# First-layer products of the coupling net: from f32 to three f16 passes, with the low part made on VectorE

## The reference

```python
def _coupling_net(h, w1, b1, w2, b2, w3, b3, w4, b4):
    h = _gelu(h @ w1 + b1)           # 128 -> 128
    h = _gelu(h @ w2 + b2)           # 128 -> 64
    h = _gelu(h @ w3 + b3)           # 64 -> 32
    return jax.nn.sigmoid(h @ w4 + b4)   # 32 -> 1
...
gf = _global_net(x.mean(axis=1, keepdims=True), ...)
out = x
for _ in range(3):
    tf = _coupling_net(out, ...)
    combined = 0.7 * gf + 0.3 * tf
    coupling = 0.1 + adaptive_range * (combined - 0.5) * 2.0
    out = out + coupling * _twist(out)   # [p_r, -p_i, -o_r, o_i]
```

## Time and profile before

| | us |
|---|---|
| median of 3 runs | 1114.27 |
| the profiled execution | 1111.88 |
| its span, first to last instruction | 1110.2 |
| TensorE busy (matmuls) | 987.5 (89%) |
| VectorE busy | 778.4 (70%) |
| ScalarE busy | 643.7 (58%) |
| GpSimd busy | 397.7 (36%) |

### The profile page before, as it was taken

The page is one execution under the profiler, slowest core; times in us unless marked ns, Lnnn a source line. Parts: engine busy times, 40 slices in busy tenths (PEclk is TensorE's granted clock), DMA queues, the critical chain, the costliest instruction groups (busy, mean ns, idle before and its releaser), DMA issues. The chain is left out here.

```text
span 1110.2 us, 30578 instructions
## 1 busy us (share of the span) xinstructions
PE 987.5 (89%) x10724; PEld 590.2 (53%) x10725; DVE 778.4 (70%) x1402; ACT 643.7 (58%) x1150; POOL 397.7 (36%) x565
## 2 busy tenths in 40 slices
PE   5479599999869999989899999999998699999996
PEld 2256488896444555546645554455545445555442
DVE  9754145553688899936677778787777888998257
ACT  3722144443437777763476667756674377777674
POOL 2154577775055555546000000000000555555312
PEclk9689699999979999999999999999998799999998
DMA  9578844642672333352000000000005633333002
GB/s 274 210 236 264 290 142 135 179 142 56 206 230 83 111 114 105 95 164 77 1 1 1 1 0 0 0 0 0 1 1 187 222 98 100 101 108 93 11 1 77
DMA packets 166651, 114.28 MB, mean 103 GB/s; under 512 B 15764, under 2 KB 160414, under 8 KB 166578
## 3 DMA queue, kind: packets, MB, share of 16 engines
q1 hardware_dynamic: 161970, 104.40, 31.3%
q0 software_dynamic: 4608, 8.93, 2.3%
HBM read 77.04 MB, written 37.29 MB: 103 GB/s over the span
## 5 line engine op out<-in xcount | busy, mean ns | idle before, releaser
L1628 ACT ACTIVATE at_p<-banks 128x512 f32<-128x512 f32 x384 | 222.8, 597 | 84.7 <-PE banks L1497 80.9
L1643 DVE TENSOR_REDUCE at_mx<-banks 128x12 f32<-128x1536 f32 x128 | 224.2, 1758 | 28.2 <-PE banks L1482 26.5
L1433 POOL TENSOR_SCALAR_AFFINE_SELECT at_p<-at_p 128x512 f32<-128x512 f32 x256 | 159.7, 636 | 138.0 <-ACT at_p L1628 131.6
L1497 PE MATMUL banks<-at_qbl,at_kst 128*128 128x512 f16 x384 | 143.1, 390 | 1.5 <-ACT at_p L1628 1.5
L2029 PE MATMUL banks<-f_h_hi,w_hi_h 128*128 128x512 f16 x256 | 97.2, 380 | 4.8 <-DVE f_h_lo L2194 2.7
L2015 POOL TENSOR_TENSOR x_res<-x_res,w_a2bo 128x512 f32<-128x512 f32 x8 | 10.2, 1275 | 254.0 <-DVE ln_z L1948 254.0
L2030 PE MATMUL banks<-f_h_lo,w_hi_h 128*128 128x512 f16 x256 | 97.0, 379 | 0.0
L2031 PE MATMUL banks<-f_h_hi,w_lo_h 128*128 128x512 f16 x256 | 97.0, 379 | 0.0
L422 POOL DMA_INDIRECT expert_rows<-xn_tok,slot x64 | 64.2, 1004 | 82.6 <-DVE slot L976 42.9
L1005 DVE TENSOR_TENSOR ex_h_sb<-ex_sg,banks 128x512 f32<-128x512 f32 x56 | 38.3, 688 | 68.4 <-ACT ex_sg L503 44.7
L1510 PE MATMUL banks<-at_p,at_va 128*32 128x256 f32 x1024 | 81.4, 379 | 0.0
(11 more groups left out here) (429 smaller groups left out, 2369.3 us busy)
## 6 DMA issues: line engine op xcount, KB each, us to landing
xnT<-kernel_padded SPq DMA_DIRECT2D x8, 1024.0 KB, 8.4
at_qst<-at_q_stacked SPq DMA_DIRECT2D x32, 256.0 KB, 3.0
at_ksc<-at_k_stacked SPq DMA_DIRECT2D x32, 256.0 KB, 3.3
at_kst<-at_k_stacked SPq DMA_DIRECT2D x32, 256.0 KB, 2.8
at_qbl<-at_q_stacked SPq DMA_DIRECT2D x128, 64.0 KB, 1.9
expert_rows<-ex_h_sb SPq DMA_DIRECT2D x1, 5760.0 KB, 18.1
gate_up_then_rows<-expert_rows SPq DMA_DIRECT2D x20, 260.0 KB, 3.1
ssm_powers<-kernel_padded SPq DMA_DIRECT2D x4, 1024.0 KB, 6.7
```

What stands on the lines that cost most here:

```text
L1433: pool.affine_select(out=blk, in_=blk, compare_op=ALU.is_ge, fill=0.0, base=0, pattern=[[0, 4], [1, P]], channel_multiplier=-1).then_inc(p ...
L1497: pe.matmul(o, kst[m][:, g, kt * P:kt * P + P], qbl[m][:, g, :, qt * P:qt * P + P], start=True, stop=True).then_inc(t_mm, 1)
L1628: act.activation(dst, k.ps[:, turn_bank(old, g * 3 + n), :].rearrange("p (j q) -> p j q", j=4), ACT.Exp, scale=scale).then_inc(p_ready, 1)
L1643: dve.tensor_reduce(mx[:, batch[1], :, g * 4:g * 4 + 4].rearrange("p n j -> p j n"), k.ps[:, score_banks(batch, g), 0:3 * P].rearrange("p ...
```

## The change

For cycles two and three the first-layer products no longer read f32. Each chunk's place in `xnT` (512 f32 for each partition) is read as 1024 f16 numbers: the first 512 hold a high part, the others a low part. ScalarE's copy writes the high part (the bank rounded to f16). VectorE then subtracts the high part from the bank and writes the low part (`low_part`, a new function; its instruction is L2612 of the new file), counted by a new semaphore `back_low`. TensorE waits for that semaphore and multiplies in three f16 passes that add up in the bank: high weights by high part, high weights by low part, low weights by high part (L2328 to L2330). The product of the two low parts is left out. The weights' parts are made once by GpSimd, with two more instructions at the end of `net_constants`. Cycle one keeps its f32 products.

Where VectorE's subtractions stand is written by hand too: those of chunks 0 to 2 of group g come after `twisted(g, y, 1)`, and that of chunk 3 of the other group comes between `twisted(g, y, 0)` and `twisted(g, y, 1)`.

```diff
--- before.py
+++ after.py
@@ -2306,7 +2306,8 @@
         self.l1_mm, self.l2_mm, self.l3_mm = ([k.sem(f"c_l{n}_mm{g}") for g in G] for n in (1, 2, 3))
         self.l4_mm, self.t_mm = [k.sem(f"c_l4_mm{g}") for g in G], [k.sem(f"c_t_mm{g}") for g in G]
         self.g1_done, self.g2_done, self.g3_done = ([k.sem(f"c_g{n}_done{g}") for g in G] for n in (1, 2, 3))
-        self.back_done = [k.sem(f"c_back{g}") for g in G]
+        self.back_done, self.back_low = ([k.sem(f"c_back{n}{g}") for g in G] for n in ("", "_low"))
+        self.w1_hi, self.w1_lo = (k.sb(f"c_w1_{n}", [P, P], F16, ctx=ctx) for n in ("hi", "lo"))
         self.prepared, self.net_mm, self.net_act = k.sem("g_prepared"), k.sem("g_pe"), k.sem("g_act")
         self.g1 = [k.sb("c_g1_0", [P, GC, CHUNK], ctx=ctx)]
         self.mean = k.sb("g_mean", [P, BATCH], ctx=ctx)
@@ -2319,9 +2320,18 @@
         return self.k.xT[:, (g * GC + c) * CHUNK:(g * GC + c + 1) * CHUNK]
 
     def layer1_product(self, pe, g, y, c):
-        if y:
-            pe.wait_ge(self.back_done[g], (y - 1) * GC + c + 1)
-        pe.matmul(self.bank(g, c), self.k.w["cw1"][:], self.chunk(g, c), start=True, stop=True).then_inc(self.l1_mm[g], 1)
+        if not y:
+            pe.matmul(self.bank(g, c), self.k.w["cw1"][:], self.chunk(g, c), start=True, stop=True).then_inc(self.l1_mm[g], 1)
+            return
+        pe.wait_ge(self.back_low[g], (y - 1) * GC + c + 1)
+        hi, lo = self.parts(g, c)
+        pe.matmul(self.bank(g, c), self.w1_hi[:], hi, start=True, stop=False)
+        pe.matmul(self.bank(g, c), self.w1_hi[:], lo, start=False, stop=False)
+        pe.matmul(self.bank(g, c), self.w1_lo[:], hi, start=False, stop=True).then_inc(self.l1_mm[g], 1)
+
+    def parts(self, g, c):
+        both = self.chunk(g, c).bitcast(F16)
+        return both[:, 0:CHUNK], both[:, CHUNK:2 * CHUNK]
 
     def layer1_gelu(self, act, g, y, c):
         act.wait_ge(self.l1_mm[g], y * GC + c + 1)
@@ -2366,10 +2376,13 @@
         n += 1
     pool.wait_ge(made, n)
     pool.tensor_scalar(net.mean[:], net.mean[:], 1.0 / SEQ, None, ALU.mult).then_inc(made, 1)
-    assert n + 1 == PREPARED
-
-
-PREPARED = 21
+    pool.tensor_copy(net.w1_hi[:], w["cw1"][:]).then_inc(made, 1)
+    pool.wait_ge(made, n + 2)
+    pool.tensor_tensor(net.w1_lo[:], w["cw1"][:], net.w1_hi[:], ALU.subtract).then_inc(made, 1)
+    assert n + 3 == PREPARED
+
+
+PREPARED = 23
 
 
 def coupling(k, net, attention, z, st):
@@ -2377,7 +2390,7 @@
 
     nc, w = k.nc, k.w
     G = range(GROUPS)
-    beta, bank, chunk = k.beta, net.bank, net.chunk
+    beta, bank = k.beta, net.bank
     l1_mm, l2_mm, l3_mm, l4_mm, t_mm = net.l1_mm, net.l2_mm, net.l3_mm, net.l4_mm, net.t_mm
     g1_done, g2_done, g3_done, back_done = net.g1_done, net.g2_done, net.g3_done, net.back_done
     tanh_done, beta_made = [k.sem(f"c_tanh{g}") for g in G], k.sem("g_beta")
@@ -2517,7 +2530,7 @@
 
         def copy_back(g, y, c):
             act.wait_ge(t_mm[g], y * GC + c + 1)
-            act.activation(chunk(g, c), bank(g, c), ACT.Copy).then_inc(back_done[g], 1)
+            act.activation(net.parts(g, c)[0], bank(g, c), ACT.Copy).then_inc(back_done[g], 1)
 
         def opening():
             for p in range(2):
@@ -2593,6 +2606,11 @@
                                          op0=ALU.mult, op1=ALU.add).then_inc(factor[g], 1)
             dve.wait_ge(factor[g], made)
 
+        def low_part(g, y, c):
+            dve.wait_ge(back_done[g], y * GC + c + 1)
+            hi, lo = net.parts(g, c)
+            dve.tensor_tensor(lo, bank(g, c), hi, ALU.subtract).then_inc(net.back_low[g], 1)
+
         def products(g, y, h):
             at, own = slice(g * GT + h * HT, g * GT + h * HT + HT), slice(h * HT, h * HT + HT)
             for dst, src, s in ((0, 64, 0), (64, 0, 1)):
@@ -2630,8 +2648,13 @@
                     closing()
                 else:
                     factors(g, slice(0, GT), y + 1, y * 3 + 3)
-                    for h in range(2):
-                        twisted(g, y, h)
+                    twisted(g, y, 0)
+                    if (g, y) != (0, 0):
+                        low_part(1 - g, y - 1 + g, 3)
+                    twisted(g, y, 1)
+                if y < LAST:
+                    for c in range(GC - 1):
+                        low_part(g, y, c)
 
     def pool_program(pool):
         for g in G:
```

## The result

The changed kernel took 1123.51 us (median of four runs, 1120.54 to 1124.69), beside 1114.30 for the kernel before on the same chip (four runs, 1113.79 to 1114.49): 9.2 us more, a ratio of 1.008 with a 95% interval of 1.0067 to 1.0093. The forecast was 1122.2, with a range of 1118.8 to 1127.0.

What follows compares the result with a forecast made beforehand. TensorE was taken to bound the kernel before; after the change, a ring of waits through TensorE, ScalarE and VectorE. 0.6 + 4.0 + 1.7 = 6.3 us, plus 1.6 for the clock, gave 7.9: 1122.2 us, range 1118.8 to 1127.0.

Steps and rivals of the forecast that it cites:

- TensorE bounds the kernel before, VectorE's slack decides: In the coupling, TensorE fills each 9.54 us repetition; ScalarE and VectorE have slack, and VectorE's slack decides the change's effect.
- Product 3 waits for VectorE's subtraction of chunk 3, TensorE idle 2.7 us in each half: In each coupling half, that subtraction queues behind factors, products and first addition, so TensorE idles 2.7 us before product 3.
- A repetition of 10.86, +1.32: One repetition of the coupling takes 10.86 us instead of 9.54, 1.32 more; three repetitions add 4.0 us.
- 0.65 for three: Three f16 passes over 512 columns on TensorE take 0.65 us, against 0.96 to 1.06 for an f32 product.
- the ring: In the coupling, a loop of waits through TensorE, ScalarE and VectorE, none of them full; 6.3 us more in all.
- First half 0.6 late, last half +1.7: In the coupling's first half product 0 ends 0.6 us late; in its last half product 3 ends 1.7 us later.
- One fall of the clock, +1.6: TensorE's clock drops to 1.2 GHz once after an idle stretch in the coupling, costing 1.6 us; zero to four possible.
- The rival with a fall in every half: TensorE's clock falls in all four coupling halves: 13.1 us more, 1127.4 us; chance 0.15 for every or nearly every half.
- GpSimd: Two added 128x128 instructions on the constants fit into GpSimd's idle 1.32 us before its first mask: cost 0, at most 0.5.
- Subtractions free of GpSimd, factors not: During GpSimd's 4.52 us additions to x_res, VectorE's subtractions cost nothing extra; factors wait 0 to 0.3 us each, taken as 0.

Runs made afterwards that it cites:

- The filled kernel: The changed kernel with twelve f16 passes of 512 columns, their result unread, put on TensorE between products 2 and 3 of each half; median 1123.66 us, ratio 1.0078.
- the f32 waits: The changed kernel with f32 copies and products as before, VectorE's subtractions writing to an unread spare tile and TensorE still waiting for them; median 1130.49 us, ratio 1.0141.
- the earlier subtraction: The changed kernel with the subtraction of chunk 3 moved up one VectorE instruction, ahead of the first addition; median 1122.41 us, ratio 1.0048.

## Why the prediction was right, point by point

- **TensorE bounds the kernel before, VectorE's slack decides.** Right. The experiment on the order moves one VectorE instruction and the repetition goes from 11.13 to 9.88.
- **Product 3 waits for VectorE's subtraction of chunk 3, TensorE idle 2.7 us in each half.** Right: 2.64 to 2.65, four times, ended by it each time. The hand-overs inside came out as worked out. The factors start 0.30 behind the end of the tanh (1077.38), where it was 0.03 before, so the subtraction of chunk 2 costs them 0.27 (0.26 forecast); the subtraction of chunk 3 starts 1.14 behind the first addition and takes 0.69. Product 3 starts 5.61 behind the end of product 0 (E+5.66 forecast).
- **A repetition of 10.86, +1.32.** The mechanism was right, the size too small: 11.13, +1.59. The mis-sized term is the f16 triple, "0.65 for three" from the earlier trace rows. That is the distance between the starts of two triples when they follow one another. In the ring product 0's triple counts until ScalarE can read it: from its first pass at 1075.03 (1075.00 in the timeline) to the gelu's start at 1075.86 it takes 0.83 to 0.86: the passes start 0.22 apart, but the last one, recorded with 0.38, must end. Product 3, behind an idle stretch, takes 0.75 to the next matmul's start (1070.31 to 1071.06). Together some 0.28 a repetition, about the whole of the miss of 0.27. It went into the sum as 6.3 where 7.4 was measured.
- **First half 0.6 late, last half +1.7.** 0.74 and 1.85, each off by 0.12 to 0.15 for the same reason: a triple counts until its last pass has ended.
- **One fall of the clock, +1.6.** One fall costs 1.55 to 1.65, as estimated; the number was two in one execution and three in another. The filled kernel's trace has none, so the idle stretches are needed for them as far as the traces show, and they account for 3.3 us of the profiled run. The reading of the earlier trace rows, one fall in two such stretches, was a fair one: over the four traces with such stretches (the kernel after twice, the f32 waits, the earlier subtraction) sixteen idle times of 1.38 to 2.65 us were followed by nine falls, none of them behind the two stretches of 1.38. The rival with a fall in every half came in none of the profiled executions.
- **GpSimd.** The two added instructions on the constants take 0.29 and 0.43, and the first mask still waits for ScalarE (kernel after, GpSimd's timeline; it answers to the earlier trace rows), so they cost nothing that shows:

```profile
885.50 0.29 POOL L2379 CAST c_w_hi<-w_cw 128x128 f16<-128x128 f32 x1
885.88 0.43 POOL L2381 TENSOR_TENSOR c_w_lo<-w_cw,c_w_hi 128x128 f16<-128x128 f32 x1
...
887.71 1.36 POOL L1433 TENSOR_SCALAR_AFFINE_SELECT at_p<-at_p 128x512 f32<-128x512 f32 x2 [1.40 <-ACT at_p L1628]
```

- **Subtractions free of GpSimd, factors not.** Right on both. In the kernel after two subtractions ran at full pace inside a GpSimd addition, while the factors just missed it (VectorE, then GpSimd):

```profile
1098.17 1.29 DVE L2612 TENSOR_TENSOR xnT<-banks,xnT 128x512 f16<-128x512 f32 x2 [1.54 <-ACT xnT L2533]
```

```profile
1096.78 4.54 POOL L2664 TENSOR_TENSOR x_res<-x_res,xn_tok 128x2048 f32<-128x2048 f32 x1 [7.95 <-DVE xn_tok L2630]
```

  Two subtractions of 0.69, overlapped, are 1.29, and they start 1.4 behind GpSimd. The prediction read this off the addition at 913.16, which stands inside two masks that run from 912.62 to 913.84 in the trace before. The rule of the Trainium skill (SBUF — State Buffer, "Who interferes with whom") held wherever the two met here: instructions with one operand in a bank passed, factor instructions with both in SBUF waited, 2.10 instead of 0.23 at the most.
- **Where the sum came out.** Predicted +7.9, made of 6.3 for the ring and 1.6 for the clock. The medians differ by 9.2; the profiled stretch by 10.6, made of 7.4 and 3.2. Both terms were too small, the ring by 1.1 and the clock by half. That the medians still came within 1.3 us of the forecast is in part luck: the profiled run was the slowest of four, a second set of the same kernel lies 1.0118 above the kernel before (some 13 us), and how many falls the runs without a profile had is not known.

What is open: why the same idle stretch brings the clock down in one half and not in the next, why filling the stretches does not show in the runs, and why the runs of the kernel with chunk 3 in f32 lie above its trace. No version here can be told from the kernel before as faster. The nearest, chunks 1 and 2 in f16, is 1.1 us shorter in its coupling by the trace and 0.9992 (0.9972 to 1.0013) by the runs.

## What to carry to other kernels

A saving on the engine that bounds a loop is worth what its feeders allow: follow each new operand back through the engines that make it, in their queue order, and compare when it is ready with when the shortened engine gets there. On such a ring count a group of matmuls to the moment when its reader can start (0.83 to 0.86 here), not by the spacing of groups (0.65). And price the idle time that appears on TensorE twice: once as waiting, and once as the clock it may cost, 1.55 to 1.65 us a fall here, in some executions and not in others.

## What was not expected of the hardware

- The clock is not a fixed cost of a program: two falls in one execution and three in another with the same idle stretches of 2.64 to 2.65 us, and none in the one trace in which twelve f16 passes of no use filled them.
- A factor instruction, with both operands in SBUF, waited for the end of the GpSimd addition that was running, however small it was itself (16 elements a row: 0.23 alone, up to 2.10), and with the addition in pieces of 1.24 us two of them in a row waited for one piece each.
- Making the halves shorter brought the factors under GpSimd's addition, which they had missed: a wait that costs nothing in the kernel after took 0.95 and 0.65 of the 1.25 won in two of the repetitions of the kernel with the earlier subtraction.
